# Cross-attention kernel: VectorE subtracts the shift of both key tiles in step 8 of each unit, tiles in natural order in steps 8 and 9

## What is computed

```python
q, k, v = heads(layernorm(x), Wq), heads(layernorm(ctx), Wk), heads(layernorm(ctx), Wv)   # 8 heads of 64
scores = einsum('bhqd,bhkd->bhqk', q, k) / sqrt(64)
attn = softmax(scores, axis=-1)
x = x + einsum('bhqk,bhkd->bhqd', attn, v) @ W_o.T + b_o
```

## Time and profile before

| what | value |
|---|---|
| median of 3 runs | 2241.34 us (2240.20 to 2241.77) |
| the profiled execution's own time | 2239.28 us |
| its span in the trace | 2237.5 us |
| PE busy | 2200.4 us (98%), 14088 matmuls |
| DVE busy | 1718.5 us (77%) |
| ACT busy | 1088.5 us (49%) |
| POOL busy | 1586.4 us (71%) |
| granted TensorE clock, mean | 0.998 |

### The profile page before, as it was taken

How to read it: one execution, slowest core, us unless ns; L and a number is a source line. 1 busy time by engine, 2 the same in 40 slices (tenths; PEclk the granted TensorE clock), 3 DMA queues, 4 the chain that set the end, 5 groups by cost and what they waited for, 6 DMA issues and landing times.

```text
span 2237.5 us, 35987 instructions
## 1 busy us (share of the span) xinstructions
PE 2200.4 (98%) x14088; PEld 1275.1 (57%) x14088; DVE 1718.5 (77%) x2120; ACT 1088.5 (49%) x1386; POOL 1586.4 (71%) x1038
## 2 busy tenths in 40 slices
PE   8999999999999999999999999999999999999997
PEld 8998865555555555555555555555555555544774
DVE  6866556888888888888888888888888888863776
ACT  4654434444544444445445444454454454453454
POOL 1200027888888888888888888888888888888332
PEclk9999999999999999999999999999999999999999
DMA  7750236777777777777777777777777777787844
GB/s 271 229 172 10 76 87 141 158 162 157 160 162 157 166 169 172 171 168 169 171 164 167 171 169 171 169 165 169 164 162 167 164 165 166 164 183 157 264 153 150
DMA packets 171627, 365.45 MB, mean 163 GB/s; under 512 B 30329, under 2 KB 76537, under 8 KB 170946
## 3 DMA queue, kind: packets, MB, share of 16 engines
q0 software_dynamic: 59904, 218.13, 48.0%
q1 hardware_dynamic: 111554, 145.02, 20.1%
HBM read 95.82 MB, written 49.04 MB: 65 GB/s over the span
## 4 chain that ended last, share of the span: by engine, by line
PE 93%; DMA 2%; issue 1%; ACT 1%; POOL 1%; DVE 1%; SPq 0%; DVEq 0%; ACTq 0%; POOLq 0%
PE ps L1478 33%; PE ps L1354 11%; PE ps L1455 8%; PE ps L1457 8%; PE ps L1459 8%; PE ps L1447 4%; PE ps L1310 4%; PE ps L1542 4%; PE ps L1321 3%; PE ps L1331 3%; DMA acca<-pt 1%; PE ps L1282 1%; POOL accp L611 1%; PE ps L1359 1%; PE ps L1487 1%
## 5 line engine op out<-in xcount | busy, mean ns | idle before, releaser
L798 ACT ACTIVATE pt<-ps 128x1024 f32<-128x1024 f32 x800 | 777.9, 1021 | 884.6 <-PE ps L1459 873.7
L611 POOL TENSOR_TENSOR accp<-accp,pt 128x1024 f32<-128x1024 f32 x416 | 1044.1, 2510 | 193.1 <-ACT pt L798 191.8
L1002 DVE TENSOR_REDUCE mx_part<-ps 128x2 f32<-128x1024 f32 x768 | 938.1, 1221 | 290.2 <-PE ps L1354 290.2
L1478 PE MATMUL ps<-pt,v 128*64 128x512 f32 x3328 | 805.6, 605 | 0.0
L1096 DVE TENSOR_TENSOR ps<-ps,shb 128x1024 f32<-128x1024 f32 x403 | 493.2, 1224 | 49.7 <-PE ps L1459 49.6
L1478 PEld LDWEIGHTS ps<-pt,v 128*64 128x64 f32 x3328 | 201.8, 136 | 344.6 <-issue 338.2
L1354 PE MATMUL ps<-kk,qh 64*128 64x512 f32 x1520 | 339.2, 444 | 1.7 <-DVE mx_part L1002 1.6
L1354 PEld LDWEIGHTS ps<-kk,qh 64*128 64x128 f32 x1520 | 140.9, 183 | 340.5 <-DVE mx_part L1002 257.7
L1455 PE MATMUL ps<-qh,kk 64*128 64x512 f32 x1664 | 328.3, 390 | 3.5 <-ACT pt L798 3.4
L1457 PE MATMUL ps<-qh,kk 64*128 64x512 f32 x1664 | 328.5, 390 | 0.0
L1459 PE MATMUL ps<-ql,kk 64*128 64x512 f32 x1664 | 328.1, 389 | 0.0
(11 more groups left out here) (164 smaller groups left out, 1765.1 us busy)
## 6 DMA issues: line engine op xcount, KB each, us to landing
acca<-pt POOLq DMA_DIRECT2D x224, 512.0 KB, 4.9
accb<-pt POOLq DMA_DIRECT2D x160, 512.0 KB, 4.6
q_scratch<-kk SPq DMA_DIRECT2D x32, 512.0 KB, 4.3
acca<-accp POOLq DMA_DIRECT2D x32, 512.0 KB, 4.6
o_scratch<-ost SPq DMA_DIRECT2D x32, 512.0 KB, 3.1
og<-o_scratch SPq DMA_DIRECT2D x32, 512.0 KB, 5.9
shb<-m_scratch SPq DMA_DIRECT2D x31, 512.0 KB, 4.7
xs<-x SPq DMA_DIRECT2D x16, 512.0 KB, 6.1
```

The lines of the kernel that those rows point to most:

```text
L611: nc.gpsimd.tensor_tensor(acc[:, :], acc[:, :], pt[n % PT_SLOTS][:, :], ALU.add).then_inc(added_p, 1)
L798: nc.scalar.activation(pt[n % PT_SLOTS][:, :], src, ACT.Exp, scale=SCALE).then_inc(exped, 1)
L1002: nc.vector.tensor_reduce(mx_part[w % 2][:, m % QT, :, m // QT], ps[:, b:b + 2, :], AX_X, ALU.max)\
L1478: ins = mm(ps[HD * h:HD * (h + 1), 6, :], v[:, t, f:f + HD], pt[n % PT_SLOTS][:, h * QB:(h + 1) * QB], start=(t == 0), stop=(t == NT - 1))
```

## The change

In step 8 (`J_BOTH`) of units 1 to 31 the even tile, 16, gets its shift from DVE too, and PE's shift pair for it is gone. In step 8 and in step 9 PE does its tiles in natural order: all of the even tile, then all of the odd one (step 9 keeps its shift pair for tile 18 and DVE's subtraction for tile 19). On DVE step 8 becomes: reduce maximum 24, subtract from tile 16, reduce maximum 25, subtract from tile 17, then `row_max`. The waits on ACT and DVE follow the new order (`nth_scored`, `nth_added`).

```diff
@@ -65,14 +65,34 @@
+J_BOTH = 8
+
+
 def added(u, t):
 
-    return u > 0 and t % 2 == 1
+    return u > 0 and (t % 2 == 1 or t == 2 * J_BOTH)
+
+
+def odd_first(u, j):
+
+    return u > 0 and j not in (J_BOTH, J_BOTH + 1)
 
 
 def tiles_added(u):
 
-    return NJ * max(u - 1, 0)
+    return (NJ + 1) * max(u - 1, 0)
+
+
+def nth_added(u, t):
+
+    return tiles_added(u) + t // 2 + (2 if t > 2 * J_BOTH else 1)
+
+
+def nth_scored(u, t):
+
+    if not odd_first(u, t // 2):
+        return NT * u + t + 1
+    return NT * u + (t if t % 2 else t + 2)
@@ -775,9 +795,9 @@
                 if added(u, t):
-                    act.wait_ge(shifted, tiles_added(u) + t // 2 + 1)
+                    act.wait_ge(shifted, nth_added(u, t))
                 else:
-                    act.wait_ge(scored, n + 2 if added(u, t + 1) else n + 1)
+                    act.wait_ge(scored, nth_scored(u, t))
@@ -1092,7 +1112,7 @@
-                dve.wait_ge(scored, NT * u + t)
+                dve.wait_ge(scored, nth_scored(u, t))
@@ -1111,12 +1131,17 @@
                     for w, m in todo[:1]:
                         take_max(w, m)
+                    both = u > 0 and j == J_BOTH
                     if added(u, 2 * j + 1):
-                        add_shift(u, 2 * j + 1)
+                        add_shift(u, 2 * j if both else 2 * j + 1)
                     for w, m in todo[1:]:
                         take_max(w, m)
+                        if both:
+                            add_shift(u, 2 * j + 1)
                         if m == NM - 1:
                             row_max(w)
+                    if both and len(todo) < 2:
+                        add_shift(u, 2 * j + 1)
@@ -1509,15 +1534,19 @@
-                    elif added(u, 2 * j + 1):
+                    elif odd_first(u, j):
                         open_tile(u, 2 * j)
                         shift_scores(u, 2 * j, True)
                         open_tile(u, 2 * j + 1)
                         scores(u, 2 * j + 1, True, True)
                         scores(u, 2 * j, False, True)
                     else:
-                        score_tile(u, 2 * j)
-                        score_tile(u, 2 * j + 1)
+                        for t in (2 * j, 2 * j + 1):
+                            if added(u, t):
+                                open_tile(u, t)
+                                scores(u, t, True, True)
+                            else:
+                                score_tile(u, t)
```

## The result

The changed kernel takes 2250.45 us, the median of 8 runs (2248.21 to 2252.96); the kernel before, run beside it, 2241.11 (8 runs). The ratio is 1.0042, with an interval of 1.0033 to 1.0051: +9.3 us, slower. The forecast was 2255.0, from 2245 to 2261.

What follows compares the result with a forecast made beforehand. The prediction took PE to bound the kernel. Units 1 to 29 at +0.47 (13.6), unit 30 at +0.33 and unit 31 at -0.2 made +13.7 us, so a median of 2255.0 us, range 2245 to 2261.

Steps and rivals of the forecast that it cites:

- What bounds the kernel: PE sets each step; the wait of step 10's first maxima for DVE's second reduction is there but hidden by 0.08 us.
- The removed pair: PE's shift pair of tile 16 in step 8, on the path: 0.23 us less in each of 31 units, 7.1 in all.
- Wait 1: Step 9: PE's opening of tile 19 waits 0.23 us for exponential 17, and an uncovered weight load adds 0.10.
- Wait 2: First maxima of step 10 wait 0.37 us for DVE, whose subtraction 19 and second reduction now follow tile 19.
- No further `open_tile` waits.: After tile 19, PE opens no later tile late: exponential 19 done at about 8.62, tile 21 opened after 9.2; no price.
- unit 30: No maxima from step 9 on, so only the wait at tile 19 remains, 0.46 + 0.10: +0.33 us.
- unit 31: No maxima in step 8 either; exponential 17 is done within 0.1 us of PE's need: -0.2 us.
- The sum: All units together, +13.7 us: 13.6 from units 1 to 29, +0.33 from unit 30, -0.2 from unit 31.
- 29 units at +0.47: Units 1 to 29, steps 8 to 9: -0.23 + 0.23 + 0.10 + 0.37 = +0.47 us each, 13.6 in all.
- B: Rival: only the wait of step 10's maxima, exponential 17 being 0.46 us earlier; +0.14 per unit, +3.6, 2245.0 us; chance 0.07.
- C: Rival, faster: both waits in step 9 and before step 10 stay covered, 31 x 0.23 gained, 2234.2 us; chance 0.04.
- D: Rival: DVE's three hand-overs each come 0.09 us later in the new order; +21.5, 2262.8 us; chance 0.04.

## Why the prediction was right

**What bounds the kernel.** PE, with DVE's second reduction 0.03 to 0.08 us from being a bound: right. Natural order in one step, with nothing else changed, was enough to bring it out.

**The removed pair, 0.23.** Right: step 9 begins at 3.85, and the kernel with both reductions short is at 8.03.

**Wait 1, 0.23 and an uncovered load of 0.10.** Right: tile 19 starts at 5.32 for 5.33. The load idles 0.47 (forecast about 0.5) and the pair behind it comes after 0.34 (1231.66 to 1232.00 in the trace). The release from DVE to ACT, for which no row stood, is 0.04: subtraction 17 ends at 1230.54 and the exponential starts at 1230.58.

**Wait 2, 0.37.** Right in place; PE alone would have been ready at 8.31 (the kernel with maximum 1 short), not 8.36, so the waiting is 0.43, and the sum is unchanged, as DVE sets the end. The load idles 1.24; the forecast had said near 1.2.

**"No further `open_tile` waits."** This step failed for units 30 and 31. It was worked out for a unit with maxima in step 10. In unit 30 there are none: PE, freed of wait 2, comes to tile 21 earlier and finds exponential 19 not done. PE at the end of step 9 and in step 10 of unit 30:

```profile
2000.27 0.50 PE L1480 MATMUL ps<-qh,kk 64*128 64x512 f32 x2 [0.27 <-ACT pt L818]
...
2003.03 0.49 PE L1472 MATMUL ps<-sh,ones_row 64*128 64x512 f32 x2
2003.62 0.50 PE L1480 MATMUL ps<-qh,kk 64*128 64x512 f32 x2
```

From a shift pair that begins a step to the next pair 0.33 is usual, here it is 0.59, and the uncovered load comes on top. This is why unit 30 is +0.6 and not +0.33. In unit 31 steps 8 to 10 come to +0.2 and not to -0.2; the transfer's -2.3 and -2.5 ahead of them hide that.

**The sum.** +13.7 was forecast for the whole, +9.3 and +9.8 were measured. The term that carries it, 29 units at +0.47, was right: steps 8 and 9 cost 0.47 in both profiles of the changed kernel. (The whole units come to 54.90 and 54.85, against 54.42 and 54.43; the 0.05 that the second profile lacks lies in other steps.) Of the 4 us between, about 2 are unit 31, which the sum had at -0.2 and which came out at -2.1 and -2.3: ScalarE's wait for the transfer of tile 1 was not in the sum at all. Unit 30 takes 0.3 of that back. Another 1 us or more is the clock: at equal granted clock the kernels differ by 10.0 to 12.7 us, not by 9.3. The rest, 1 to 1.5 us, is unassigned, and about as large as what the other steps of units 1 to 29 differ by from one pair of profiles to the other. So the forecast's mechanism and its main term hold, and the total came out under the forecast for reasons that it did not name.

**The rivals.** B needed exponential 17 to be 0.46 earlier; the kernel with maximum 25 short makes it 0.48 earlier, and lands on B's position (8.42 for 8.40). Its time is +0.7 us where B had +3.6; unit 31 is short by 2.1 in it as well. C, the faster outcome, needed both waits covered, and it came when both were taken away, not before. D: on this chain every instruction of DVE that follows another directly starts 1.14 or 0.61 after the start of the one before, that is 0.08 to 0.09 inside it, and 8.74 leaves no room for 0.27 more. The Trainium skill (VectorE: DVE Perf Modes, The DRAIN you can't avoid) says that the next operation does not start until the pipe is empty, but it adds there that one which is not held starts earlier. The prediction took up the first sentence alone; the trace agrees with the second.

## What to carry to other kernels

Where one engine is 98% busy and another 77%, the busy shares do not say that moving work to the second is free. In this kernel it would have been free only if its results had not been needed sooner than they came. Follow one result through the engines, with the instructions queued ahead of it, up to the point at which the first engine waits for it. Here a chain of eight links, two of them reductions that have nothing to do with the moved work, set the length of two steps, and DVE was idle for 0.64 us in the middle of it. A wait that is covered by less than 0.1 us, as DVE's second reduction was here, is to be counted as a wait before any change of order.

## What was not expected of the hardware

The copy of tile 1 into `acca` in the last unit lands after 4.4 us instead of 6.25, and is waited for 1.85 us less, after a change that does nothing to it and slows the units before; it is the same in two profiles of each kernel. And a dip of the granted clock to the lower level ahead of unit 0 came and went between two profiles of the same program; the first unit began 2.7 us later with it (314.7 against 312.0).
